# A GRU, two mixtures of experts and a sampled sequence on one core: gathered rows and sums in buffers of their own, heads of 31 steps with tails of 7 in two passes, and the indirect DMAs one to a step

## The reference, cut to what matters

```python
# layer 0: a GRU over 512 steps
r = sigmoid(i_r + h_r); z = sigmoid(i_z + h_z); n = tanh(i_n + r * h_n)   # i = x_t @ W_ih + b_ih, h_ = h @ W_hh + b_hh
h = (1 - z) * n + z * h
# ... then a base matmul and LoRA experts, 2 of 8 by a router
x = x + base(hs) + sum_e w_e * lora_e(hs)
# layer 1: the features resampled at places given by a grid (linear, along D), then 2 of 8 experts
v = w0 * x[..., i0] + w1 * x[..., i1]
top_vals, top_idx = top_k(v @ gate_w.T + gate_b, 2); routing = softmax(top_vals)
for e in range(8):
    h = v @ w1[e].T + b1[e]
    y = h[:, 0::2] * sigmoid(1.702 * h[:, 0::2]) * (h[:, 1::2] + 1)
    out += (y @ w2[e].T + b2[e]) * routing_of(e)
x = x + out
```

## Time and profile before

| | |
|---|---|
| median of 3 runs | 1867.83 us (1867.08 to 1871.98) |
| the profiled execution, its own time | 1871.95 us |
| its span, first to last instruction | 1870.2 us |
| granted clock of PE, mean | 0.995 |
| busy: PE, weight loads, DVE, ACT, POOL | 1692.0, 1151.0, 1298.3, 782.6, 300.5 us |
| chain that ended last: PE, DVE, ACT, issue, SP's queue, DMA | 66, 16, 6, 5, 3, 3 % |
| first step of the GRU ends, last step ends | 32.8 us, 1668.8 us |
| DMA traffic | 334.06 MB, 179 GB/s in the mean |

### The profile page before, as it was taken

One profiled execution on the slowest core, in us unless ns is written; L12 is line 12 of the kernel. 1 busy time (PEld: TensorE's weight loads), 2 busy tenths in 40 slices (PEclk: granted clock), 3 DMA queues, 4 the chain that ended last, 5 costly groups with the idle time before them and its releaser, 6 DMA issues.

```text
span 1870.2 us, 95461 instructions
## 1 busy us (share of the span) xinstructions
PE 1692.0 (90%) x40986; PEld 1151.0 (62%) x40986; DVE 1298.3 (69%) x5788; ACT 782.6 (42%) x2714; POOL 300.5 (16%) x600
## 2 busy tenths in 40 slices
PE   5888888878889999989799999989899999988997
PEld 4777777666556666656566666656566666654444
DVE  6888788887767776767777767677677777763323
ACT  5655566643334344333333434432334343323442
POOL 2222222221211110121211101121311111022001
PEclk9999999999999999999999999999999999999999
DMA  7436445444436667525336666436246666349994
GB/s 257 144 134 215 156 158 191 167 156 149 139 94 193 202 206 216 171 84 146 125 106 203 194 212 212 145 85 166 99 141 193 204 195 193 118 124 392 376 350 135
DMA packets 176690, 334.06 MB, mean 179 GB/s; under 512 B 46449, under 2 KB 46601, under 8 KB 176265
## 3 DMA queue, kind: packets, MB, share of 16 engines
q1 hardware_dynamic: 171144, 311.17, 51.9%
q0 software_dynamic: 5120, 16.78, 2.8%
HBM read 263.10 MB, written 64.78 MB: 175 GB/s over the span
## 4 chain that ended last, share of the span: by engine, by line
PE 66%; DVE 16%; ACT 6%; issue 5%; SPq 3%; DMA 3%; DVEq 0%; POOL 0%; ACTq 0%
PE bank_g L682 16%; PE bank L968 14%; PE bank_g L687 12%; PE bank_g L698 7%; PE bank L988 7%; DVE xt L1440 5%; DVE na L1446 3%; DVE pre L1442 3%; ACT rz L1114 3%; DVE hs_early L1452 3%; ACT seq_h L1114 3%; PE bank L724 2%; DMA wih<-x_rows 1%; PE bank L964 1%; PE bank L950 1%
## 5 line engine op out<-in xcount | busy, mean ns | idle before, releaser
L1842 POOL COPY hxs<-hs 128x32 f16<-128x32 f16 x512 | 224.3, 438 | 1320.6 <-DVE hs L1460 1318.5
L1114 ACT ACTIVATE rz<-pre 128x32 f32<-128x32 f32 x512 | 126.6, 247 | 729.5 <-DVE pre L1442 728.5
L682 PE MATMUL bank_g<-whh,hs_early 128*32 128x256 f16 x8192 | 318.2, 275 | 122.8 <-DVE hs_early L1452 118.7
L1440 DVE STREAM_TRANSPOSE xt<-bank_g 128x256 f32<-128x256 f32 x512 | 230.6, 450 | 207.1 <-PE bank_g L687 197.1
L682 PEld LDWEIGHTS bank_g<-whh,hs_early 128*32 128x32 f16 x8192 | 171.4, 95 | 313.2 <-DVE hs_early L1452 303.4
L698 PE MATMUL bank_g<-whh,hs 128*32 128x128 f16 x16384 | 324.4, 219 | 11.0 <-issue 10.8
L687 PE MATMUL bank_g<-whh,hs 128*32 128x256 f16 x8192 | 313.1, 273 | 0.1
L968 PE MATMUL bank<-wm,wih 128*128 128x512 f16 x1272 | 309.6, 381 | 3.2 <-issue 2.5
L698 PEld LDWEIGHTS bank_g<-whh,hs 128*32 128x32 f16 x16384 | 257.2, 97 | 16.8 <-issue 15.4
L687 PEld LDWEIGHTS bank_g<-whh,hs 128*32 128x32 f16 x8192 | 203.2, 96 | 22.8 <-DVE hs L1460 3.2
L1114 ACT ACTIVATE seq_h<-na 128x16 f32<-128x16 f32 x512 | 115.5, 226 | 208.2 <-DVE na L1446 207.8
(11 more groups left out here) (245 smaller groups left out, 2027.7 us busy)
## 6 DMA issues: line engine op xcount, KB each, us to landing
wm<-moe_split SPq DMA_DIRECT2D x318, 512.0 KB, 4.4
wm<-in_w_moe SPq DMA_DIRECT2D x32, 768.0 KB, 5.4
moe_split<-wm SPq DMA_DIRECT2D x32, 768.0 KB, 5.1
wih<-x_rows SPq DMA_DIRECT2D x58, 256.0 KB, 4.6
y_rows<-wih SPq DMA_DIRECT2D x58, 256.0 KB, 4.6
whh<-moe_split SPq DMA_DIRECT2D x24, 512.0 KB, 7.7
gi<-moe_split SPq DMA_DIRECT2D x18, 512.0 KB, 7.9
xr<-in_x SPq DMA_DIRECT2D x16, 512.0 KB, 4.7
```

What stands on the lines that cost most here:

```text
L682: mm(out_strip(0, j, 2 * P), early_cols[:, 8 * B * k:8 * B * (k + 1)], strip(whh[:, 1, k, 0:2 * D], j), start=(k == 0), stop=False)
L1114: return nc.scalar.activation(dst, src, func, **kw)
L1440: link(V.transpose(rows, bank_g[0][:, 0:2 * P].rearrange("p (m c) -> p m c", c=32)))
L1842: Q.tensor_copy(hxs[:, par, :, :, :, col].rearrange("p s k b -> p s (k b)"), hs_new).then_inc(S["h_kept"], 1)
```

## The change

It has these parts.

- **Buffers.** `xr` and `x1` take turns as `sums[f]`: x is loaded there and the sum is made in place. Gathered rows of passes 0 to 2 go to units of the `wih` buffer that are free (GOT_UNITS). The weights of the tokens (`tpr`) have two buffers. So the load of x no longer waits for the gathered rows to be used; that of the last pass is issued in slot 13 of pass 2. `store_out` moves from the head to slot 0.
- **Heads and tails.** HEADS = (31, 31, 29, 29), TAILS = (7, 7, 9, 9).
- **Scatters** of passes 0 and 1: one behind each of eight steps. **Gathers** of passes 0 and 1: five in the tail, one a step, three in the next head behind steps 0, 2 and 4; with them three of the four scalings, combines, and all turn-backs and sums go to the next head (steps by the tables; turn-backs and sums in its last four). Idle matmuls are set anew. Pass 2 keeps its pairs, nine-step tail and work in it.
- **mixt** is copied by ACT in slot 0 in all passes, behind the last turn-back.
- **The last pass.** Weights of tiles 0 and 1 are asked for before the GRU ends (after the gathers of pass 2 have landed). The stores of pass 2 stand between the weight loads. Rows of tiles 2 and 3 are loaded by ACT's queue in slot 0. `add_held` goes by output rows k for all tokens at once, the bias product too, and the stores go by k.
- **The start.** b_hh's row is loaded once, behind the three parts of W_hh, and is cast and split after them; `bias_f` isn't cleared any more.

```diff
-HEAD = 29
-TAIL = 9
+HEADS = (31, 31, 29, 29)
+TAILS = tuple(FT - n - NT * SLOT for n in HEADS)
...
-SCATTER = {19: (0,), 20: (1,), 21: (2, 3), 22: (4,), 23: (5, 6), 24: (7,)}
-GATHER = {FT - TAIL + 2 + b: (2 * b, 2 * b + 1) for b in range(B)}
-IDLE = {26: 5, 27: 4, FT - TAIL + 2: 5, **{FT - TAIL + i: 3 for i in (7, 8)}}
+SCATTER_EACH = {19 + n: (n,) for n in range(2 * B)}
+SCATTER_PAIRS = {19: (0,), 20: (1,), 21: (2, 3), 22: (4,), 23: (5, 6), 24: (7,)}
+GATHER_EACH = {FT - 5 + n: (n,) for n in range(5)}
+GATHER_PAIRS = {FT - 7 + b: (2 * b, 2 * b + 1) for b in range(B)}
+GATHER_LATE = {0: 5, 2: 6, 4: 7}
+IDLE_HEAD = {28: 5}
+IDLE_TAIL = {FT - 5: 5, FT - 2: 4, FT - 1: 4}
+GOT_UNITS = ((2, 7), (5, 8), (6, 0), (11, 1))
+SCALED_TAIL, COMBINE_TAIL = {5: 0}, {6: 0}
+SCALED_HEAD, COMBINE_HEAD = {0: 1, 6: 2, 12: 3}, {5: 1, 20: 2, 24: 3}
+def late(f):
+    return f < FB - 2
...
-        got = [[xr_f[:, b * D:(b + 1) * D], x1s_f32[:, b * D:(b + 1) * D]] for b in range(B)]
+        sums = [(xr, x1)[f % 2] for f in range(FB)]
+        got = [[[unit(i).bitcast(F32) for i in GOT_UNITS[b]] for b in range(B)] for _ in range(FB - 1)] + \
+              [[[v[:, b * D:(b + 1) * D] for v in (xr_f, x1s_f32)] for b in range(B)]]
...
-            sp.wait_ge(S["bias_zero"], 1)
-            for row in range(2):
-                sp.dma_start(bias_f[32 * row:32 * row + 1, :].rearrange("o (m p) -> o m p", m=K),
...
             for q in range(3):
                 sp.dma_start(part_of(wm32[1], q), part_of(w_hh, q)).then_inc(whh_in[q], 16)
+            sp.dma_start(bias_f.rearrange("o (m p) -> o m p", m=K), b_hh[:, 2 * K:].rearrange("p (o m) -> o m p", o=1),
...
             def load_block(f, q):
-                if q == 0 and f:
-                    sp.wait_ge(S["back_mm"], f * B)
-                    sp.wait_ge(S["combined"], f * B)
-                    for b in range(B):
-                        sp.wait_ge(gathered[b], f * 32)
-                elif q == 0:
+                if q == 0 and f > 1:
+                    sp.wait_ge(S["out_stored"], 32 * (f - 1))
+                if q == 0 and f == 0:
...
                 if s == 19:
                     sp.wait_ge(S["scattered"], (f + 1) * B * 2 * 16)
+                    if f:
+                        sp.wait_ge(S["combined"], f * B)
...
             def load_slot(f, j, u):
+                if j == 0 and u < 2 and f:
+                    store_out(f - 1, u)
+                if j == NT - 2 and u >= 4 and g == FB - 1:
+                    load_block(g, u - 4)
...
             f = FB - 1
-            sp.wait_ge(S["h_ready"], FB * FT + 1)
-            for q in range(2):
-                load_block(f, q)
-            for q in range(2):
-                store_out(f - 1, q)
-            for j in range(LAST_RING):
+            for b in range(B):
+                sp.wait_ge(gathered[b], f * 32)
+            for j in range(2):
                 for n in range(K):
                     load_up(f, j, n)
                 for n in range(2):
                     load_down(f, j, n)
+            sp.wait_ge(S["h_ready"], FB * FT + 1)
+            for j in range(2, LAST_RING):
+                for n in range(K):
+                    load_up(f, j, n)
+                for n in range(2):
+                    load_down(f, j, n)
+                store_out(f - 1, j - 2)
             sp.wait_ge(S["scattered"], FB * B * 2 * 16)
-            load_rows(f, 2)
-            load_rows(f, 3)
...
+                if f and s >= HEADS[f] - B:
+                    if s - HEADS[f] + B == 0:
+                        pe.wait_ge(S["x2_lo"], (f + 1) * B)
+                        pe.wait_ge(S["slots_done"], f + 1)
+                    turn_back(f - 1, s - HEADS[f] + B, back[f - 1])
...
+            def add_bias(f, k):
+                mm(added[k][:, :], b2w[:, k * P:(k + 1) * P], mixt[:, :, :].rearrange("e b n -> e (b n)"),
+                   start=True, stop=False, skip_group_check=True)
+            def add_held(f, i, k):
+                pe.wait_ge(S["held_lo"], i + 1)
+                for w, a in PARTS:
+                    r = mm(added[k][:, :], held_y[i][:, a, k], held_t[i][:, w].rearrange("p b n -> p (b n)"),
+                           start=False, stop=(i == HELD - 1 and a == 1), skip_group_check=True)
...
-            act.wait_ge(S["bias_row_in"], 16 * 2)
-            act.wait_ge(S["bias_zero"], 2)
-            run(bias_n[0:2 * 32], bias_f, ACT.Copy, scale=WS).then_inc(S["bias_hi"], 1)
             whh_hi(1)
...
                 gi_out(0, m)
+            act.wait_ge(S["bias_row_in"], 16)
+            act.wait_ge(S["bias_zero"], 1)
+            run(bias_n[0:1], bias_f, ACT.Copy, scale=WS).then_inc(S["bias_hi"], 1)
             x_hi(2)
...
                     run(ys[:, 0], yf, ACT.Copy).then_inc(S["y_hi"], 1)
+                    if f == FB - 1 and j == 0:
+                        act.wait_ge(S["scattered"], FB * B * 2 * 16)
+                        for n in (2, 3):
+                            act.dma_start(xg[n % 2], x_rows[n * P:(n + 1) * P]).then_inc(rows_in[n % 2], 16)
...
             def x1_sum(f, o):
                 if o == 0:
                     dve.wait_ge(S["block_in"], (f + 1) * 32)
-                    if f:
-                        dve.wait_ge(S["out_stored"], f * 32)
...
+                    after_gru = gru_on and f > 0 and s in GATHER_LATE
+                    if gru_on and (s in scatters or s in gathers or after_gru):
                         pool.wait_ge(S["gates_mm"], 2 * (g * FT + s + 2))
+                    if after_gru:
+                        gather(f - 1, GATHER_LATE[s])
```

263 lines of the change are left out of this document (139 added, 124 removed).

## The result

The changed kernel takes **1848.51 us** (median of six runs, 1846.92 to 1849.99), the kernel before 1868.51 beside it: a ratio of 0.9891, 95% interval [0.9874, 0.9908], 20.0 us less. The forecast was 1847, with a range of 1839 to 1860. The execution that was profiled took 1848.49 us with a span of 1846.7.

What follows compares the result with a forecast made beforehand. The recurrence's loop of PE, DVE, ACT and DVE bounds the kernel at 3.14 us a step. Terms -4.1, -7.4, -2.1, +1.2, -2.7, -5.0, -0.7 sum to -20.8, from median 1867.83 to 1847 us, range 1839 to 1860.

Steps and rivals of the forecast that it cites:

- The tails: Last steps of passes 0 and 1: one gather a step and combines moved out remove the excess, -7.4 us.
- rival B: Gathers and scatters: each indirect DMA costs its step something wherever it stands; -14.1 us in all, 1854; chance 0.10.
- What comes back: Next heads, after the tails' work moves there: late gathers free, combines and turn-backs lengthen steps, +1.2 us together.
- The turn-backs' 0.6: Head's last step: PE's four turn-backs plus first expert tile's five matmuls cost 0.3 us in each of two heads.
- The combines' 0.6: Next heads: four DVE combines a pass, alone in their steps, overfill the hole by 0.07 us each, eight times.
- The start: First step: w_hh loads issued ahead of b_hh's row gain 4.8 us, the row's split costs 0.7; -4.1 us.
- rival C: Start: the wait moves, as the bias row is late behind 3 MB of w_hh; -16.7 us in all, 1851; chance 0.10.
- The sum with x: Last pass, first sum: x in its own buffer no longer waits for the previous pass's stores, -2.7 us.
- Rows 2 and 3: Last pass, tile 2: early weights and row loads through ACT remove PE's wait and slow matmuls, -5.0 us.
- Rival A: Last pass: weights still fill the queues, so tile 2 starts as late; -15.8 us in all, 1852; chance 0.17.
- The end: Final sums by output rows, still eight stores: half of at most 1.3 us from the stores, -0.7 us.
- Rival D: Heads: PE's clock falls where side work is gone; 16 slot steps lose 27 us, 1874, slower; chance 0.02.

## Why the prediction was right, and where it was not

**The tails**, -7.4 forecast and -7.4 measured. The reason given (a second gather runs over the step's end while PE has its gate products) is shown by the pairs put back and by the gathers at chosen places; rival B (each indirect DMA costs its step something) is out, since single ones stand in steps of 3.13 us. The reading behind it was loose in one point: PE's gap of 0.37 us begins at 1239.85, 0.08 us behind the end of the gather that the prediction put beside it (1239.77). How the 7.4 is shared between pairs and late combines was not measured. The runs speak for a share of the combines on the second chip, where a scatter pair's crossing costs nothing and pass 2's tail still has 2.4 us of its 3.5 us of excess: in one of its steps of 4.10 us the combine is on DVE from 1639.63 to 1640.38, and the transposition follows it.

**The scatters**, -2.1 forecast, -2.1 without the one long step.

**What comes back**, +1.2 forecast, about +0.9 measured, spread over the heads as said above. The turn-backs' 0.6 came as 0.19 and 0.27, a step later than forecast: the last two steps of both heads last 3.13, but in the first slot step the products of the first expert tile are still on PE when h is ready, and the gate products start late (at 939.21, 0.64 us behind h at 938.57, where it is 0.36 elsewhere). The combines' 0.6 came as 0.44 in steps 0 to 18, with the late gathers and scalings, but not evenly: in the tail of pass 1 one ends at 1245.78, and the transposition follows 1.03 us behind h instead of 1.02; in the head of pass 2 the step of one lasts 3.49, and why was not tried.

**The start**, -4.1 forecast, -2.6 measured: the term was sized by ACT's idle time of 4.79 us, when the limit was the transfer. The queues carried next to nothing for 3.6 us, and w_hh could come earlier by about that; -3.8, +0.7 for the bias row (as forecast) and +0.4 for x's cast, a small piece of rival C, gives -2.7. An unchanged start differs by 1.2 us between ten profiles, so the tenths mean little.

**The sum with x**, -2.7 and -2.7 (0.30 us of wait are left where 3.06 were).

**Rows 2 and 3**, -5.0 and -5.1, but not for the reason given alone, so that the agreement is in part luck. 3.3 us is the wait, for which either the early weights or ACT is enough, and which needs both undone to come back as 2.45. It isn't worth its size: with both undone the kernel is 1.0 us slower, since the waits of the last tiles shrink in return. 1.7 us is the clock. The second drop at tile 2 came in none of the twelve runs; the first, at tile 0's products, came in the first profile of the changed kernel and in none of the twelve. Whether the kernel before has both in most executions is not known, for only one of it was profiled. But that one wasn't poor in clock: its mean granted clock was 0.995, and that of 21 more executions of the kernel before was 0.988 to 0.997, 0.994 in the mean, where ten of the changed kernel had 0.997 or 0.998. So fewer clock drops are a part of what the change brings, though the prediction counted only the one at tile 2. Why the profiles differ by 23.5 us and the medians by 20.0 stays open. Rival A didn't come.

**The end**, -0.7 forecast, -2.6 from tile 2 on: missed by the step that looked at the stores only. PE's waits for x_rows in the last tiles fell from 4.6 to 2.1 us, which is 2.5 of it. The sum by output rows and the eight stores are worth little: SP issues them in 4.40 us instead of 6.53, but from the last but one of the second products' groups of twelve (1847.56 before, 1824.41 now) to the end of the span it is 22.6 us before and 22.3 now.

**Rival D.** The clock did fall in the heads of pass 2 in some runs (at 1323.4 with the row moved, at 1320.7 for 10.2 us with the fills, as at 1336.0 in the kernel before), and in the head of pass 1 with pairs put back (920.7), always behind scatter pairs: in 4 of the 18 heads with pairs in the fourteen profiles, and in none of the 24 with single ones. In tails it fell at 1243.9 before and at 1244.9 with pairs put back, and in none with single gathers. So single ones make such a drop rarer, the opposite of what the rival feared.

The Trainium skill (SBUF — State Buffer, Who interferes with whom) has TensorE wait for nobody; here PE's products stop for 0.44 us at the end of a gather on POOL and not beside fills on POOL. Where the cost showed, the measurement speaks against that rule, and it decides; that the cause is a port is not shown. On the second chip, where a gather at the same place cost nothing, the rule would stand.

Still open: what differs between the chips; by what way a gather holds back PE and the transposition; which of x, the stores and `add_held` made most of the last pass's gain; what the long steps at the start wait for.

## What to carry to other kernels

In a chain of short steps, look at where in the step an indirect DMA is written, not at how many there are: one in the quiet half is free, one beside the chain's own matrix products can cost up to 1.15 us. Size a gain from an earlier load by how long the queues carried next to nothing, not by how long the reader was idle. A wait that is taken away can be paid again later: undo the edit and look at the time to the end, not only at the wait. And before a term is taken from a profile, ask whether other executions show it too: the clock drop at tile 2 was in the one profile of the kernel before, and how often it comes there is not known.

## What the runs showed of the hardware

- A step with an indirect DMA on POOL from 0.5 to 1.5 us behind h, and 0.1 us of another ahead of it, took 4.29 and 4.31 us instead of 3.13 on one chip; one at that place alone cost 0.00 on another. 15 and 19 chained fills on POOL cost nothing on the first.
- One row of 512 packets of 4 bytes was issued in 0.81 us, but a load of 1 MB behind it needed 8.26 us to be issued, and landed at 24.96 us, where it landed at 22.33 with the row behind it.
- The granted clock was 0.50 for stretches of 3.41 us (6.83 and 10.24 were seen too), at places that differ between two profiles of one kernel: in the changed one from 26.7 and 1685.6 us in the first, from 28.5 and nowhere in the last pass ahead of PE's last product in the second.
- A stretch in which the queues carried x and the stores moved 186 GB/s at a busy share of 0.97; with weight loads in their place it was 364 GB/s at 1.03.
